# Conditioned attention over 32 batches: a fixed cycle per batch replaced by calls written out for each batch

## The reference

```python
def layer0(x, emb):                                # 8 heads of 32
    xn = ln(x); q, k, v = xn @ Wq, xn @ Wk, xn @ Wv
    q = softmax(q, axis=-1); k = softmax(k, axis=1)          # q over its features, k over the tokens
    att = einsum('bnhd,bnhl->bhdl', k, v)
    y = einsum('bnhd,bhdl->bnhl', q, att)
    scale, shift = split(silu(emb) @ W_emb + b_emb, 2)
    return x + silu(ln(y) * (1 + scale) + shift) @ W_out + b_out
def layer1(x, emb):                                # 16 heads of 16
    xn = ln(x); q, k, v = xn @ q_w, xn @ k_w, xn @ v_w
    att = softmax(einsum('bnhl,bmhl->bnmh', q, k), axis=m)   # 256x256 for each head
    y = einsum('bnmh,bmhl->bnhl', att, v)
    ...                                            # norm, scale and shift, silu, out_w, + x as above
return layer1(layer0(x, cond), cond)
```

## Time and profile before

| what | value |
|---|---|
| median of 3 runs | 958.85 us (958.46 to 960.41) |
| the profiled execution | 959.34 us, of which its span is 957.5 us |
| PE busy | 852.1 us (89%) |
| DVE busy | 821.8 us (86%) |
| POOL busy | 739.6 us (77%) |
| ACT busy | 698.3 us (73%) |
| DMA moved | 83.76 MB, 35.7% of 16 engines' span |

### The profile page before, as it was taken

One profiled execution on the slowest core, in us unless ns is written; L12 is line 12 of the kernel. 1 busy time (PEld: TensorE's weight loads), 2 busy tenths in 40 slices (PEclk: granted clock), 3 DMA queues, 4 the chain that ended last, 5 costly groups with the idle time before them and its releaser, 6 DMA issues.

```text
span 957.5 us, 25672 instructions
## 1 busy us (share of the span) xinstructions
PE 852.1 (89%) x8715; PEld 614.1 (64%) x8715; DVE 821.8 (86%) x1678; ACT 698.3 (73%) x1236; POOL 739.6 (77%) x1212
## 2 busy tenths in 40 slices
PE   3866688899999999999999999999999998888774
PEld 1755576566777777777777777777777775554432
DVE  7869859899999999999999999999999998777732
ACT  0222364588888888888888888888888888778763
POOL 9345898788988888889888888888888877765221
PEclk9577899899999999999999999999999999999977
DMA  7111143434444544344434434343334332333100
GB/s 206 23 30 38 36 101 90 92 92 93 91 103 102 103 87 103 97 99 103 103 98 90 98 98 102 91 91 90 96 103 103 103 81 81 81 101 103 39 25 33
DMA packets 140090, 83.76 MB, mean 87 GB/s; under 512 B 78262, under 2 KB 132636, under 8 KB 139964
## 3 DMA queue, kind: packets, MB, share of 16 engines
q1 hardware_dynamic: 139964, 82.13, 35.7%
HBM read 39.52 MB, written 25.79 MB: 68 GB/s over the span
## 4 chain that ended last, share of the span: by engine, by line
DVE 38%; PE 33%; issue 17%; POOL 9%; ACT 1%; SPq 1%; DMA 1%; DVEq 0%; POOLq 0%; ACTq 0%
PE banks L696 10%; DVE NM L1061 10%; DVE st L962 6%; PE banks L683 4%; PE banks L664 4%; POOL XB L1777 4%; PE banks L607 3%; PE banks L541 3%; PE banks L618 3%; DVE wemb L1101 2%; DVE Y L1085 2%; DVE V L1003 2%; DVE V1t L1053 2%; DVE qm L992 2%; DVE km L976 2%
## 5 line engine op out<-in xcount | busy, mean ns | idle before, releaser
L1061 DVE TENSOR_REDUCE NM<-banks 128x4 f32<-128x1024 f32 x256 | 304.0, 1216 | 28.0 <-PE banks L664 25.4
L1582 ACT ACTIVATE wraw<-banks,uu 128x1024 f32<-128x1024 f32 x154 | 170.4, 1117 | 32.5 <-PE banks L683 31.7
L1754 POOL TENSOR_TENSOR SH<-ST,SH 128x512 f16<-128x512 f32 x64 | 84.5, 1320 | 52.5 <-ACT SH L1550 52.5
L1582 ACT ACTIVATE PX<-banks,uu 128x1024 f32<-128x1024 f32 x102 | 113.1, 1116 | 14.7 <-PE banks L683 14.2
L664 PE MATMUL banks<-SK,SQ 51*128 51x256 f16 x1024 | 100.5, 273 | 24.1 <-DVE V L1003 11.1
L541 PE MATMUL banks<-wo,SH 128*128 128x256 f16 x768 | 96.6, 284 | 14.5 <-POOL SH L1754 13.4
L683 PE MATMUL banks<-SQ,SK 53*128 53x256 f16 x1024 | 95.6, 274 | 6.2 <-DVE NM L1061 1.8
L541 PE MATMUL banks<-wv,ZT 128*128 128x256 f16 x768 | 98.5, 280 | 0.0
L1700 POOL TENSOR_TENSOR rs<-ve,nhalf 128x2 f32<-128x2 f32 x128 | 89.4, 698 | 10.6
L541 PEld LDWEIGHTS banks<-wo,SH 128*128 128x128 f16 x768 | 74.9, 101 | 33.0 <-POOL SH L1754 14.6
L696 PE MATMUL banks<-wraw,V 128*32 128x256 f32 x1232 | 88.6, 388 | 3.0 <-ACT wraw L1582 2.1
(11 more groups left out here) (186 smaller groups left out, 2012.8 us busy)
## 6 DMA issues: line engine op xcount, KB each, us to landing
scr<-AB SPq DMA_DIRECT2D x64, 256.0 KB, 3.0
X<-in_x_dram SPq DMA_DIRECT2D x32, 256.0 KB, 2.8
SK<-scr SPq DMA_DIRECT2D x64, 128.0 KB, 3.0
SQ<-scr SPq DMA_DIRECT2D x64, 128.0 KB, 2.7
out_dram<-wemb SPq DMA_DIRECT2D x32, 256.0 KB, 3.1
SK<-scr SPq DMA_DIRECT2D x64, 64.0 KB, 2.9
SQ<-scr SPq DMA_DIRECT2D x64, 64.0 KB, 2.7
wemb<-in_L_cond_W_emb_dram SPq DMA_DIRECT2D x1, 1024.0 KB, 5.5
```

Source lines behind the costliest of these rows:

```text
L1061: V.tensor_reduce(NMe[:, c, :, 2 * g:2 * g + 2], banks[:, n:n + 2, :].rearrange("p a (h m) -> p a h m", m=T), AX.X, ALU.max, negate=True). ...
L1582: A.activation(px(v % 5), banks[:, n:n + 2, :].rearrange("p a n -> p (a n)"), ACT.Exp, scale=uu[:, 0:1]).then_inc(S["exp"])
L1754: G.tensor_tensor(SH[:, l, 1], ST[:, l], SH[:, l, 0], ALU.subtract).then_inc(S[f"sl{l}"])
```

## The change

The loops go. In their place each of the five queues has a list of calls for all 32 batches, written out one after the other, in one order that need not be the same for any two batches. From about batch 3 to batch 25 the lists do repeat with a period of one batch. `BANK[g]` becomes a string with a digit for each batch, and `FREED[g]` names for each batch the read, with its count, that frees the bank. The setup pieces are in other places. No piece is added or taken away, and none has other instructions, but for one wait that `parts` on POOL gains. The diff, cut to its core (the period shown is the one around batch 13):

```diff
 BANK = {
-    "gk0": 3, "gkt": 3, "gq0": 2, ... "gr0": 4,
+    "gk0": "47026001237173737373737373737373",
+    "gr0": "64464240404040404040404040402406",
...
-HELD = {
...
+FREED = {
+    "gk0": (
+        "q1:1 mx_b Y0:1 film0 q1:3 ka:1 Y0:6 vt:3 ka:5 exp:20 max:38 max:47 ..."),
...
 SETUP = {
     "PE": (
-        "pm tr_w0 ar_w0 row1 row0 row3 col cnd bb1 tr_w1 fm0 ar_w1 tr_o1 bb0 tr_b tr_o0 ar_o1 ar_o0 tr_f0 "
-        "row2 ar_f0 fm1 ar_b bb2 tr_f1 ar_f1 ").split(),
+        "tr_o0 tr_o1 pm cnd ar_o1 ar_o0 fm0 row0 row3 row2 tr_w0 row1 fm1 tr_w1 col ar_w0 bb0 bb1 tr_f0 tr_b "
+        "ar_b bb2 tr_f1 ar_f1 ar_f0 ar_w1 ").split(),
     "DVE": (
-        "mb0 w0m mx_w0 perm w0p fr1 csl w1m bm mc csT p3 wl_q0 mx_w1 wl_v0 wl_k0 o1m bc1 fr0 w1p bc0 o0m "
+        "o1m o0m csl mb0 mc mx_o1 mx_o0 csT o1p o0p w0m w1m fr0 perm mx_w0 wl_o0 wl_o1 fr1 w0p f0m bc0 bc1 p3 "
...
     "POOL": (
-        "cst fill nmz v1z ").split(),
+        "fill nmz cst v1z ").split(),
 }
...
-            for before in HELD[g]:
-                for name, k, a in before:
...
+            for before in FREED[g].split()[b].split("+"):
+                name, _, n = before.partition(":")
+                if n:
+                    e.wait_ge(S[name], int(n))
+                elif name != "-":
+                    ready(e, name)
...
@@ tensor
+            y1T(10); qtT(17); rows(13, 0); rows(13, 1); pv(11, 5); y0(17); v1p(13); cols(11, 7); v0(18); ktT(18)
+            pv(11, 6); cols(12, 0); pv(11, 7); rows(13, 2); rows(13, 3); att(18); cols(12, 1); o1(10); cols(12, 2)
+            rows(13, 4); cols(12, 3); ty(11, 1); y0T(16); rows(13, 5); rows(13, 6); rows(13, 7); pv(12, 0)
@@ vector
+            st0(17); max_(14, 7); np_(14); q1(19); qm(19); nt(14); km(20); x1(17); rk(20); rq(19); Y1_(13, 0)
+            s2(17); max_(15, 0); Y0(19); st1(12); max_(15, 1); vt(15); v(20); s1(19); max_(15, 2); max_(15, 3)
+            at_(20); s0(22); o_(12); max_(15, 4); Y1_(13, 1); max_(15, 5); s3(13); max_(15, 6); st0(18)
@@ scalar
+            exp(13, 1); exp(13, 2); exp(13, 3); th0(17); yt(13, 0); sh0(17); qa(16); ka(16); exp(13, 4); yt(13, 1)
+            ke(20); qe(19); exp(13, 5); exp(13, 6); qt(19); th1(12); yt(13, 2); exp(13, 7); sh1(12); kt(20)
@@ gpsimd
             def parts(b, l, src):
+
+                turns[l] += 1
+                e.wait_ge(S[f"z{1 - l}"], turns[1 - l])
...
+            fill(); nmz(); cst(); xb0(0); v1z(); r0(0); z0(0); xb0(1); r0(1); z0(1); qs(0); r0(2); z0(2); r0(3)
...
+            yn1(29); sl1(29); r3(30); yn1(30); sl1(30); r3(31); yn1(31); sl1(31)
```

More of the change, by code:

```diff
@@ L578, in ktT @@
                 clear(e, "gkt", b)
[L579 removed]
+                transposes(home("gkt", b), KE).then_inc(S["ktT"])
             def q0(b):
@@ L712, in y1T @@
                 clear(e, "gy1T", b)
-                transposes(BANK["gy1T"], YN[:, 1]).then_inc(S["y1T"])
+                transposes(home("gy1T", b), YN[:, 1]).then_inc(S["y1T"])
             def o1(b):
@@ new lines, in _ @@
+            tr_o0(); tr_o1(); pm(); cnd_t(); ar_o1(); ar_o0(); fm0(); row0(); row3(); row2(); tr_w0(); row1()
+            fm1(); tr_w1(); col(); ar_w0(); bb0(); bb1(); tr_f0(); tr_b(); q0(0); v0(0); ar_b(); bb2(); v0(1)
+            k0(0); k0(1); qtT(0); q0(1); tr_f1(); ktT(0); ar_f1(); att(0); ktT(1); ar_f0(); y0(0); ar_w1(); qtT(1)
+            att(1); k0(2); v0(2); y0(1); q0(2); k0(3); v0(3); q0(3); y0T(0); k0(4); v0(4); ktT(2); q0(4); qtT(2)
+            att(2); o0(0); y0(2); ktT(3); y0T(1); qtT(3); att(3); y0(3); y0T(2); o0(1); ktT(4); qtT(4); att(4)
@@ new lines, in _ @@
+            q1(6); np_(0); qm(6); vt(2); nt(0); max_(1, 0); max_(1, 1); rk(6); st0(5); at_(6); max_(1, 2)
+            max_(1, 3); rq(6); km(7); Y0(6); max_(1, 4); max_(1, 5); v(7); max_(1, 6); q1(7); s1(6); max_(1, 7)
+            qm(7); np_(1); rk(7); s0(9); nt(1); rq(7); at_(7); Y1_(0, 0); max_(2, 0); max_(2, 1); Y0(7)
+            max_(2, 2); max_(2, 3); max_(2, 4); s1(7); Y1_(0, 1); s3(0); km(8); max_(2, 5); max_(2, 6); max_(2, 7)
+            rk(8); np_(2); x1(5); s2(5); nt(2); st1(0); max_(3, 0); Y1_(1, 0); max_(3, 1); vt(3); max_(3, 2)
@@ new lines, in _ @@
+            s1(9); max_(5, 2); max_(5, 3); at_(10); s0(12); o_(2); max_(5, 4); Y1_(3, 1); max_(5, 5); s3(3)
+            max_(5, 6); st0(8); max_(5, 7); np_(5); q1(10); qm(10); nt(5); km(11); x1(8); rk(11); rq(10)
+            Y1_(4, 0); s2(8); max_(6, 0); Y0(10); st1(3); max_(6, 1); vt(6); v(11); s1(10); max_(6, 2); max_(6, 3)
+            at_(11); s0(13); o_(3); max_(6, 4); Y1_(4, 1); max_(6, 5); s3(4); max_(6, 6); st0(9); max_(6, 7)
+            np_(6); q1(11); qm(11); nt(6); km(12); x1(9); rk(12); rq(11); Y1_(5, 0); s2(9); max_(7, 0); Y0(11)
@@ new lines, in _ @@
+            st1(4); max_(7, 1); vt(7); v(12); s1(11); max_(7, 2); max_(7, 3); at_(12); s0(14); o_(4); max_(7, 4)
+            Y1_(5, 1); max_(7, 5); s3(5); max_(7, 6); st0(10); max_(7, 7); np_(7); q1(12); qm(12); nt(7); km(13)
+            x1(10); rk(13); rq(12); Y1_(6, 0); s2(10); max_(8, 0); Y0(12); st1(5); max_(8, 1); vt(8); v(13)
+            s1(12); max_(8, 2); max_(8, 3); at_(13); s0(15); o_(5); max_(8, 4); Y1_(6, 1); max_(8, 5); s3(6)
+            max_(8, 6); st0(11); max_(8, 7); np_(8); q1(13); qm(13); nt(8); km(14); x1(11); rk(14); rq(13)
@@ new lines, in _ @@
+            Y1_(7, 0); s2(11); max_(9, 0); Y0(13); st1(6); max_(9, 1); vt(9); v(14); s1(13); max_(9, 2)
+            max_(9, 3); at_(14); s0(16); o_(6); max_(9, 4); Y1_(7, 1); max_(9, 5); s3(7); max_(9, 6); st0(12)
+            max_(9, 7); np_(9); q1(14); qm(14); nt(9); km(15); x1(12); rk(15); rq(14); Y1_(8, 0); s2(12)
+            max_(10, 0); Y0(14); st1(7); max_(10, 1); vt(10); v(15); s1(14); max_(10, 2); max_(10, 3); at_(15)
+            s0(17); o_(7); max_(10, 4); Y1_(8, 1); max_(10, 5); s3(8); max_(10, 6); st0(13); max_(10, 7); np_(10)
@@ new lines, in _ @@
+            s3(10); max_(12, 6); st0(15); max_(12, 7); np_(12); q1(17); qm(17); nt(12); km(18); x1(15); rk(18)
+            rq(17); Y1_(11, 0); s2(15); max_(13, 0); Y0(17); st1(10); max_(13, 1); vt(13); v(18); s1(17)
+            max_(13, 2); max_(13, 3); at_(18); s0(20); o_(10); max_(13, 4); Y1_(11, 1); max_(13, 5); s3(11)
+            max_(13, 6); st0(16); max_(13, 7); np_(13); q1(18); qm(18); nt(13); km(19); x1(16); rk(19); rq(18)
+            Y1_(12, 0); s2(16); max_(14, 0); Y0(18); st1(11); max_(14, 1); vt(14); v(19); s1(18); max_(14, 2)
@@ new lines, in _ @@
+            max_(16, 0); Y0(20); st1(13); max_(16, 1); vt(16); v(21); s1(20); max_(16, 2); max_(16, 3); at_(21)
+            s0(23); o_(13); max_(16, 4); Y1_(14, 1); max_(16, 5); s3(14); max_(16, 6); st0(19); max_(16, 7)
+            np_(16); q1(21); qm(21); nt(16); km(22); x1(19); rk(22); rq(21); Y1_(15, 0); s2(19); max_(17, 0)
+            Y0(21); st1(14); max_(17, 1); vt(17); v(22); s1(21); max_(17, 2); max_(17, 3); at_(22); s0(24); o_(14)
+            max_(17, 4); Y1_(15, 1); max_(17, 5); s3(15); max_(17, 6); st0(20); max_(17, 7); np_(17); q1(22)
@@ new lines, in _ @@
+            s3(17); max_(19, 6); st0(22); max_(19, 7); np_(19); q1(24); qm(24); nt(19); km(25); x1(22); rk(25)
+            rq(24); Y1_(18, 0); s2(22); max_(20, 0); Y0(24); st1(17); max_(20, 1); vt(20); v(25); s1(24)
+            max_(20, 2); max_(20, 3); at_(25); s0(27); o_(17); max_(20, 4); Y1_(18, 1); max_(20, 5); s3(18)
+            max_(20, 6); st0(23); max_(20, 7); np_(20); q1(25); qm(25); nt(20); km(26); x1(23); rk(26); rq(25)
+            Y1_(19, 0); s2(23); max_(21, 0); Y0(25); st1(18); max_(21, 1); vt(21); v(26); s1(25); max_(21, 2)
@@ new lines, in _ @@
+            max_(21, 3); at_(26); s0(28); o_(18); max_(21, 4); Y1_(19, 1); max_(21, 5); s3(19); max_(21, 6)
+            st0(24); max_(21, 7); np_(21); q1(26); qm(26); nt(21); km(27); x1(24); rk(27); rq(26); Y1_(20, 0)
+            s2(24); max_(22, 0); Y0(26); st1(19); max_(22, 1); vt(22); v(27); s1(26); max_(22, 2); max_(22, 3)
+            at_(27); s0(29); o_(19); max_(22, 4); Y1_(20, 1); max_(22, 5); s3(20); max_(22, 6); st0(25)
+            max_(22, 7); np_(22); q1(27); qm(27); nt(22); km(28); x1(25); rk(28); rq(27); Y1_(21, 0); s2(25)
@@ L1500, in _ @@
+            max_(31, 6); Y1_(29, 1); max_(31, 7); s3(29); np_(31); o_(28); nt(31); Y1_(30, 0); st1(29); Y1_(30, 1)
+            s3(30); o_(29); Y1_(31, 0); st1(30); Y1_(31, 1); s3(31); o_(30); st1(31); o_(31)
         @block.scalar
@@ L1685, in _ @@
+            sh1(30); yt(31, 3); th1(31); sh1(31)
         @block.gpsimd
```

845 lines of the change are left out of this document (452 added, 393 removed), and 192 rows, old and new, of tables (BANK, FREED, HELD).

## The result

The changed kernel takes 1010.25 us in the median of 4 runs (1009.86 to 1011.45), against 959.63 for the kernel before beside it. The ratio is 1.053, with a 95% interval of 1.051 to 1.055. The profiled execution has a span of 1008.6 us, 51.1 more than before's 957.5.

The account below looks back on a forecast made before the run. PE's own work was taken to bound the steady stage, at 25.04 us per cycle. Span 957.5 - 2 (head) + 19 (steady) - 14 (tail) = 960.5, plus 1.84 around it, median 0.5 lower: 962 us forecast, range 945 to 984.

Parts of the forecast that it names:

- What bounds the kernel now: Steady cycles before the change: PE's own work sets 25.04 us, with one 0.42 us wait for v each.
- Steady stage: 21 repeating cycles: three rings through the queues lengthen the period, the longest 25.95 us, costing +19 us.
- The ACT and DVE ring: Repeating cycle: sh0 to th1 on ACT, st1 to st0 on DVE, back to sh0; summed to 25.7 us.
- the one through PE and the bank of `gr1`: Repeating cycle: exp(·,6), gr1's bank, pv5, y0, v1p, rows2, max_(·,2); 25.95 us, taken as the longest.
- rival B: Steady cycles: the rings are not the longest path, period again 25.04, total 943 us; chance 0.11.
- Head: Start to rows(4,0): PE starts late but POOL's denser work makes it up; -2 us, from +10 to -9.
- rival C: Start of the kernel: PE's 22 us late start is not caught up, +10 instead of -2, 974 us; chance 0.12.
- Tail: rows(25,0) to the end: last maxima at 136 instead of 143.1, then 37 instead of 44.1; -14 us.
- What stays: Whole kernel: busy times stay, writing out the loops adds or removes no instruction, the new parts wait costs 0.
- A: rows(25,0) to the last maxima: PE alone binds, its idle time goes, -11.5 us more, 950; chance 0.17.
- E: Whole kernel: the written order repeats the old one and only names change, so no effect; chance of same 0.12.
- D: Repeating cycle: DVE and POOL hold each other in the ring, 0.64 us per cycle, +13 us, 975; chance 0.13.

Follow-up runs that it names:

- e5: Kernel before with its order and fixed banks, calls written out and FREED naming fewer waits: 955.17 us, ratio 0.994.
- e8: e2 with seven kinds of pieces shifted one or two places, above all rows(b,1) later on PE: 937.51 us, ratio 0.977.
- e4: Changed kernel with rows(b,2) of batches 4 to 25 two places earlier in PE's list: 999.5 us, ratio 1.040.
- e9: Changed kernel with eight kinds of pieces shifted one or two places and banks named anew: 984.07 us, ratio 1.027.
- e14: Changed kernel with 1017 bank digits replaced, same order of calls: 1010.18 us, ratio 1.051.
- e3: Changed kernel with POOL's cst moved back ahead of fill: 1010.83 us, ratio 1.053.
- e7: e2 with POOL's fill writing the same bytes as 32-bit words, half as many elements: 940.69 us, ratio 0.979.
- e10: Changed kernel with POOL's fill writing the same bytes as 32-bit words, half as many elements: 1002.62 us, ratio 1.046.
- e1: Changed kernel's calls and banks up to about 200 us, then the order and banks of the kernel before: 972.92 us, ratio 1.012.
- e11: e8 with the short fill of e7 and single pieces of the last seven batches shifted and given other banks: 921.51 us, ratio 0.962.
- e13: e5 with every bank wait of the kernel before put back, 343 more on PE: 959.82 us, ratio 1.000.
- e2: Kernel before with its order written out and a bank named per product and batch: 950.09 us, ratio 0.989.

## Why the prediction was wrong, step by step

**What bounds the kernel now: right.** PE sets the period of before, with one short wait in each cycle. e5 and e8 show how little there is to have: 24.92, then 24.58, where 25.04 less the wait of 0.42 is 24.62.

**Steady stage: a ring, but not one of the three in the sum; size wrong, +38.8 instead of +19.** The failed step is "Two more rings of the new lists, added up in the same way, are as long ... I take the longest, 25.95". The ACT and DVE ring exists (its terms add up to 25.77, not 25.7), and `sh0` waits for `st0` as foreseen. But the longest loop is none of those that I added up. The trace has one of 27.01 us, by way of `ntT` and `km`, and one of 26.73 beside it, by way of `st0` and `sh0`. The second is made of parts that I had in hand. The ring through ACT and DVE runs over `sh0`, `exp(·,6)`, `max_`, `st0`, and the one through PE and the bank of `gr1` (25.95) over `exp(·,6)`, `rows(b,1)`, `rows(b,2)`, `max_(·,2)`; by which pieces the latter closes, the prediction does not say. Where two rings cross at two points, a third one can take from each its longer part: `sh0` to `exp(·,6)` on ACT, then over the bank to PE and `rows(b,2)`, then `max_(·,2)` to `st0` on DVE. By the prediction's own durations its stretch on ACT is 9.1 us and that on DVE 10.1, where after has 9.57, the wait of 0.28 in it, and 9.98. The loop of 27.01, with `ntT` and the hold of `km` in it, is in none of my sums. My upper end of 26.4 ("rings that meet in one instruction") allowed for hand-overs only. e4 shortens the stretch on PE that both loops share and gains 11 us, and e9 gains 26 with eight shifts, 20 of them in this stage. Of the banks, e14 shows only that the digits other than that of the edge from `exp(·,6)` to `rows(·,1)` do not set the period.

**The stated test was sound.** 545 meant the rings and 526 rival B; the trace says 564.6, on the side of the rings and further.

**Head: sign wrong, +9.0 instead of -2.** Several single steps held. PE's first transpose came at 27.62 (forecast 28.8), the first `q0(0)` at 61.0 (63 to 66), `rows(0,0)` at 159.6, 12.4 later than before (forecast 11). `fm0` took its 7.04 us again, and `fm1` 3.76:

```profile
27.62 0.58 PE L866 MATMUL banks<-ident,mxw 128*1 128x128 f32 x2 [27.62 <-POOL augm L2027]
...
30.57 7.04 PE L974 MATMUL banks<-csT,wemb 128*128 128x32 f32 x32
...
43.80 3.76 PE L974 MATMUL banks<-csT,wemb 128*128 128x32 f32 x32
```

The first, 3 us behind 27.6 us without work, was as slow as in the earlier trace rows, and the second, later in the same run of PE work, was not. The two durations are as 1.87 to 1, near the two levels of 1.2 and 2.4 GHz. The Trainium skill, "TensorE: Matmul & The Clock Gate", section "What's actually happening", has the throttled clock as the default that sustained activity lifts; both rows agree with it, and what I had drawn from it for `fm0`, 3.66 us, would have been wrong, as the run had only begun.

What failed is "POOL ... is busy throughout from about 110, and `rows(0,0)` comes 11 us later than before, `rows(2,0)` 7 later, `rows(4,0)` 2 earlier". `rows(2,0)` came 11.0 later (205.5 for 194.5), and between it and `rows(4,0)` lie 48.0 us where my walk had 41.3 (from 201.5 to 242.8; before has 50.1). POOL was not the bound that I took it for: it is busy 38.3 of the 40 us from 110 to 150, but 47.0 of the 55.5 up to `rows(2,0)` and only 29.7 of the 48.0 up to `rows(4,0)`. Of the 18.9 us by which the first product of a batch is late (61.0 for 42.1), 12.4 are left at `rows(0,0)` and 9.0 at `rows(4,0)`, and my walk had made up all of them. This is rival C, the head not caught up, near its +10. Which chain holds the first four batches stays open: PE's start by itself is worth 0.3 us (e3), and a shorter `fill` helps the old order as well (e7, e10). With before's order behind it, the same head costs 13.3 (e1).

**Tail: sign wrong, +3.3 instead of -14.** The last maximum of after:

```profile
966.93 1.21 DVE L1250 TENSOR_REDUCE NM<-banks 128x4 f32<-128x1024 f32 x1
```

It ends at 968.1, 150.0 us after `rows(25,0)`; before it was 143.1, and my walk had 136. From there to the end 40.5, before 44.1, forecast 37: half of this gain was there. POOL's waits of `sl1` for `sh1` did fall, as I had read the free chains, from 52.5 us to 37.4 between 818 and 1009:

```profile
POOL SH L1955 <- ACT SH L1717: 37.4, 8, 8.7
```

That time was not on the path to the last maxima. The step that failed is "the new lists end them at 136 instead of 143.1": it took 150.0. Two thirds of that excess over before hang on the banks, which the walk did not price: e14, the same order with other digits, needs 145.4 to the last maxima and has a tail of 185.5. What holds the rest of the way for the 9 us more than my walk was not settled; e4 and e9, which shorten the steady loops, leave the tail at 190.7 and 191.6, and e1, with before's order and banks, has 183.3. e11 shows that single shifts there are worth 2.5 us (176.0 for e8's 178.5).

**What stays, costed at nothing: not quite.** The `parts` wait cost nothing that shows (e13 has it, at ratio 1.000). But "writing them out adds or removes no instruction by itself" overlooked the waits: `FREED` names fewer on PE (343 fewer in before's order) and lists them in another order, together worth 5 us (e5 against e13), and other banks are worth another 5 (e2 against e5). Both gains were measured in before's order.

**Rivals.** A and B, the faster ones, and E, no change, fell by the markers of head, period and tail. D was right in kind: the hold of `km` grew from 0.87 to 1.23 us and stands in the loop that closes last, but it can be worth at most 5.9 us there, not 13. The two effects that I had set up as alternatives, a ring (+19) and an unpaid head (+12 over the forecast), came together, and the ring's loss was twice its size; a range that lets each case stand alone can't hold that.

## What to carry to other kernels

With several in-order queues, the period is the longest loop through all of them, bank and buffer edges included; it is not enough to add up the loops that one sees, as two that cross in two places make a third. Search the loops by program, or at least join each pair at their common pieces. And a bank that is handed from one read to the next product is an edge like any data edge: it belongs into that sum. Where a product has two waits, name the one that is met last at the end.
